# Mixture-of-experts stage: order of routing work and of the experts' first steps, and the last chunk of the combination by token tiles

## The reference, cut to what matters

```python
def _L1_ffn_ref(x, router_w, router_b, w1, b1, w2, b2, sw1, sb1, sw2, sb2):
    # N = 4096 tokens, D = 256, H = 512, E = 8 experts, S = 2 shared experts, TOP_K = 2
    xf = x.reshape(-1, D)
    sh = gelu(jnp.einsum('nd,sdh->snh', xf, sw1) + sb1[:, None, :])
    shared_out = (jnp.einsum('snh,shd->nd', sh, sw2) + sb2.sum(0)) / S
    gates = xf @ router_w + router_b
    topv, topi = jax.lax.top_k(gates, TOP_K)
    probs = jax.nn.softmax(topv, axis=-1)
    comb = jnp.einsum('nke,nk->ne', jax.nn.one_hot(topi, E, dtype=xf.dtype), probs)
    h = gelu(jnp.einsum('nd,edh->enh', xf, w1) + b1[:, None, :])
    y = jnp.einsum('enh,ehd->end', h, w2) + b2[:, None, :]
    moe_out = jnp.einsum('ne,end->nd', comb, y)
    return (shared_out + moe_out).reshape(B, L, D)
...
x = x + jnp.tanh(g_ffn[1]) * _L1_ffn_ref(_layernorm(x, axis=-1), ...)
```

## Time and profile before

| | us |
|---|---|
| median of 3 runs (1161.97 to 1167.03) | 1164.91 |
| the profiled execution, its own time | 1166.86 |
| its span in the profile | 1165.3 |
| TensorE busy in the span | 1085.4 (93%) |
| VectorE | 879.2 (75%) |
| ScalarE | 697.0 (60%) |
| GpSimd | 437.8 (38%) |

### The profile page before, as it was taken

The page is one execution under the profiler, slowest core; times in us unless marked ns, Lnnn a source line. Parts: engine busy times, 40 slices in busy tenths (PEclk is TensorE's granted clock), DMA queues, the critical chain, the costliest instruction groups (busy, mean ns, idle before and its releaser), DMA issues. The chain is left out here.

```text
span 1165.3 us, 28150 instructions
## 1 busy us (share of the span) xinstructions
PE 1085.4 (93%) x9246; PEld 932.7 (80%) x9247; DVE 879.2 (75%) x1983; ACT 697.0 (60%) x1583; POOL 437.8 (38%) x571
## 2 busy tenths in 40 slices
PE   6679998999998899999999879997999999999998
PEld 4346666989887677777776559997899999999997
DVE  8699997766676788888888538886567677666776
ACT  3478996465572566676676544465565556556553
POOL 4148884631302010111102012776523233332775
PEclk9669999999999999999999887999899999999999
DMA  9646641000005355463544015896465554455675
GB/s 323 179 156 224 224 171 56 1 0 0 0 1 115 101 126 107 90 123 79 122 93 85 3 51 214 286 329 229 151 195 174 173 173 162 170 180 168 219 235 166
DMA packets 98879, 164.81 MB, mean 141 GB/s; under 512 B 12124, under 2 KB 73404, under 8 KB 96604
## 3 DMA queue, kind: packets, MB, share of 16 engines
q1 hardware_dynamic: 89260, 137.02, 39.9%
q0 software_dynamic: 9104, 26.49, 6.8%
q10 hardware_dynamic: 416, 0.04, 0.0%
HBM read 103.76 MB, written 33.69 MB: 118 GB/s over the span
## 5 line engine op out<-in xcount | busy, mean ns | idle before, releaser
L1885 DVE TENSOR_REDUCE c_mx<-d_bank 128x2 f32<-128x512 f32 x256 | 164.4, 686 | 18.4 <-PE d_bank L2037 18.0
L1800 ACT ACTIVATE c_probs<-c_t 128x512 f32<-128x512 f32 x248 | 134.7, 598 | 27.5 <-PE c_t L2063 26.7
L2986 ACT ACTIVATE d_g_full<-d_bank,d_e_bias 128x256 f32<-128x256 f32 x156 | 77.1, 494 | 102.7 <-PE d_bank L34 102.7
L32 PE MATMUL d_bank<-de_zt_hi,d_e_hi 128*128 128x256 f32 x312 | 92.0, 295 | 2.3 <-DVE de_zt_lo L2896 2.3
L33 PE MATMUL d_bank<-de_zt_lo,d_e_hi 128*128 128x256 f32 x312 | 88.6, 284 | 0.0
L34 PE MATMUL d_bank<-d_w_hi,d_g_lo 128*128 x312 | 88.3, 283 | 0.0
L33 PE MATMUL d_bank<-d_w_lo,d_g_hi 128*128 x312 | 88.2, 283 | 0.0
L1733 POOL CAST c_ct_hi<-c_c_raw 128x512 fp32r<-128x512 f32 x15 | 9.2, 611 | 210.4 <-PE c_misc L34 210.4
L32 PE MATMUL d_bank<-d_w_hi,d_g_hi 128*128 x312 | 88.2, 283 | 0.0
L34 PE MATMUL d_bank<-de_zt_hi,d_e_lo 128*128 128x256 f32 x312 | 88.1, 282 | 0.0
L3146 POOL DMA_INDIRECT d_w_lo<-d_y_rows,d_pos x64 | 65.6, 1026 | 36.2 <-DMA d_y_rows<-de_ys 17.0
(11 more groups left out here) (428 smaller groups left out, 3786.6 us busy)
## 6 DMA issues: line engine op xcount, KB each, us to landing
d_e_raw<-in_w SPq DMA_DIRECT2D x39, 514.0 KB, 3.7
a_mb<-a_maxima SPq DMA_DIRECT2D x15, 1024.0 KB, 7.6
d_w_hi<-d_zt_kept SPq DMA_DIRECT2D x26, 512.0 KB, 4.8
d_y_rows<-de_ys SPq DMA_DIRECT2D x39, 256.0 KB, 2.1
d_z_in<-d_z_rows POOLq DMA_DIRECT2D x37, 256.0 KB, 4.2
c_kt<-c_k_hi SPq DMA_DIRECT2D x64, 128.0 KB, 3.1
c_qt<-c_q_hi SPq DMA_DIRECT2D x64, 128.0 KB, 3.7
d_zt_kept<-d_w_hi SPq DMA_DIRECT2D x20, 256.0 KB, 2.6
```

The source lines that it names most:

```text
L32: tensor.matmul(out, lhs_hi, rhs_hi, start=start, stop=False)
L1800: act.activation(probs[h % PR][:], t_bank(n, p, k), ACT.Exp).then_inc(exp_done, 1)
L1885: dve.tensor_reduce(mx[n % 2][:, :, k, p:p + 1], s_ps[h % SB], AX.X, ALU.max).then_inc(max_done, 1)
L2986: act.activation(g_full[:, m, :], hid[m][:, 0:TOK], ACT.Gelu, bias=bias[u][:, m:m + 1]).then_inc(gelu_full, 1)
```

## The change

Nothing is added to or taken from the arithmetic. What moves:

- Router products: the second one (chunk 1) is issued right behind the first, ahead of the first transposes. TensorE's ranking of group 2 comes half a chunk later.
- Ranking of group 0 on VectorE: after the low part of bank 1 of chunk 2 instead of bank 3.
- First scatters: token tile 0's two are issued ahead of the fifth reciprocal root and wait for 8 GELUs instead of 12.
- Experts' turn: on TensorE behind the output of chunk 14; on VectorE behind both splits and the output of chunk 14; on ScalarE behind both splits and the exponential.
- Bias sums: four of the eight adds of the shared bias come behind tile 2's `split_w`.
- Combination: VectorE weighs chunk 14 before the output add of chunk 13; the last chunk's output is made, added and stored by token tiles, each in a bank of its own; its last gathers wait for two GELUs fewer.

```diff
@@ moe_route, scatter() and GpSimd's order @@
-            pool.wait_ge(gelu_hi, KF * (2 * group + 3) + apart)
+            pool.wait_ge(gelu_hi, KF * (2 * group + 3) + apart if i > 0 else 2 * KF)
...
         for h in range(CHUNKS):
+            if h == 2:
+                scatter(0)
             if PT * (h + 3) < TILES:
                 rstds(h + 3)
             if h >= 2 and PT * (h - 2) < TILES:
-                for i in range(PT * (h - 2), PT * (h - 1)):
+                for i in range(max(1, PT * (h - 2)), PT * (h - 1)):
                     scatter(i)
@@ ScalarE @@
-        turn_experts(act)
         split(2)
...
         split(3)
+        turn_experts(act)
@@ VectorE @@
-                if m == 3 and h % 2 == 0 and 1 <= h // 2 <= GROUPS:
+                if m == (1 if h == 2 else 3) and h % 2 == 0 and 1 <= h // 2 <= GROUPS:
                     rank(h // 2 - 1)
...
             if h == CHUNKS - 1:
-                turn_experts(dve)
+                split(2)
+                split(3)
             if h >= 1:
                 output(h - 1)
...
-        split(2)
-        split(3)
+        turn_experts(dve)
         output(CHUNKS - 1)
@@ TensorE @@
-        gates_part(0)
+        for r in range(2):
+            gates_part(r)
...
-                if r <= CHUNKS:
+                if 2 < r <= CHUNKS:
                     gates_part(r - 1)
-                if half == 0 and h % 2 == 0 and 1 <= h // 2 <= GROUPS:
+                if half == (h + 2) // MID and h % 2 == 0 and h >= 2:
                     rank(h // 2 - 1)
...
             hidden_late(h, h % 2)
-            if h == CHUNKS - 1:
-                turn_experts(pe)
             output(h - 1, (h - 1) % 2)
+        turn_experts(pe)
         output(CHUNKS - 1, (CHUNKS - 1) % 2)
@@ moe_experts, GpSimd @@
             pool.tensor_copy(w_hi[u][:], w_raw[u][:, 0:KD * FF]).then_inc(w_hi_done, 1)
+            if isinstance(i, int) and i == AHEAD:
+                add_bias(range(E // 2, E))
...
-            for e in range(E):
+            add_bias(range(E // 2))
+
+        def add_bias(some):
+            shared = out_bias[:, E, :]
+            for e in some:
                 pool.tensor_tensor(out_bias[:, e, :], out_bias[:, e, :], shared, ALU.add).then_inc(bias_shared, 1)
@@ moe_combine @@
-                after(pool, gelu_hi, KF * n + (KF // T) * t - 1)
+                after(pool, gelu_hi, KF * n + (KF // T) * (t if n < LAST else 0) - 1)
...
+        def outputs_last(t):
+            dve.wait_ge(weighed, T * TOP * CHUNKS)
+            dve.wait_ge(last_done, t + 1)
+            xs = x_all[:, T * LAST + t, :]
+            dve.scalar_tensor_tensor(out=xs, in0=y_last[t], scalar=M.half_tanh[:, 0:1], in1=xs, op0=ALU.mult,
+                                     op1=ALU.add).then_inc(last_added, 1)
...
-        for n in range(CHUNKS + 1):
-            if n < CHUNKS:
-                hidden(n)
+        for n in range(CHUNKS):
+            hidden(n)
             if n == 0:
                 probabilities()
+            if 1 <= n < LAST:
+                weigh(n - 1)
+            if n == LAST - 1:
+                weigh(n)
             if n >= 1:
-                weigh(n - 1)
                 outputs(n - 1)
+        weigh(LAST)
+        for t in range(T):
+            outputs_last(t)
```

More of the change, by code:

```diff
@@ L3099, in moe_combine @@
     HEAD = 3
+    LAST = CHUNKS - 1
     def sem(name):
@@ L3113, in moe_combine @@
     y_done, weighed, x_added = sem("y_done"), sem("weighed"), sem("x_added")
+    last_done, last_added = sem("last_done"), sem("last_added")
+    y_last = [y[LAST % 2][:, 0, :]] + [hid[t][:, 0:D] for t in range(1, T)]
     out_tiles = out.rearrange("b (j p) d -> p (b j) d", p=P)
@@ L3125, in store, with store_last @@
             sync.dma_start(out_tiles[:, T * n:T * (n + 1), :], x_all[:, T * n:T * (n + 1), :]).then_inc(x_stored, 16)
+        def store_last(t):
+            sync.wait_ge(last_added, t + 1)
+            sync.dma_start(out_tiles[:, T * LAST + t, :], x_all[:, T * LAST + t, :]).then_inc(x_stored, 16)
         sync.wait_ge(experts.y_done, S.PAIR_TILES)
@@ L3134, in on_sync @@
                 store(n - 1)
-        store(CHUNKS - 1)
-        sync.wait_ge(x_stored, 16 * CHUNKS)
+        for t in range(T):
+            store_last(t)
+        sync.wait_ge(x_stored, 16 * (CHUNKS - 1 + T))
     def on_gpsimd(pool):
@@ L3178, in hidden, with weigh_one @@
                 dve.tensor_tensor(g_lo[n % 2][:, m, :], g_full[:, m % GR, :], g_hi[n % 2][:, m, :], ALU.subtract).then_inc(gelu_lo, 1)
+        def weigh_one(n, k, t):
+            dve.wait_ge(gathered[n % RR], 16 * T * TOP * (n // RR + 1))
+            if k > 0:
+                dve.wait_ge(weighed, T * (TOP * n + k))
+            xs = x_all[:, T * n + t, :]
+            dve.scalar_tensor_tensor(out=xs, in0=rows[n % RR][:, t * TOP + k, :], scalar=M.prob[:, T * n + t, k:k + 1], in1=xs,
+                                     op0=ALU.mult, op1=ALU.add).then_inc(weighed, 1)
         def weigh(n):
-            dve.wait_ge(gathered[n % RR], 16 * T * TOP * (n // RR + 1))
             for k in range(TOP):
-                if k > 0:
-                    dve.wait_ge(weighed, T * (TOP * n + k))
                 for t in range(T):
-                    xs = x_all[:, T * n + t, :]
-                    dve.scalar_tensor_tensor(out=xs, in0=rows[n % RR][:, t * TOP + k, :], scalar=M.prob[:, T * n + t, k:k + 1], in1=xs,
-                                             op0=ALU.mult, op1=ALU.add).then_inc(weighed, 1)
+                    weigh_one(n, k, t)
+        def outputs_last(t):
[4 more added lines that the diff above has]
+                                     op1=ALU.add).then_inc(last_added, 1)
         def outputs(n):
@@ L3221, in outputs @@
                 cols = slice(t * P, (t + 1) * P)
-                out_y = y[u][:, t, :]
+                out_y = y_last[t] if n == LAST else y[u][:, t, :]
                 for m in range(KF):
@@ L3225, in outputs @@
                                       (w2_hi[:, m, :], w2_lo[:, m, :]), m == 0, m == KF - 1)
-            mm.then_inc(y_done, 1)
+                if n == LAST:
+                    mm.then_inc(last_done, 1)
+            if n < LAST:
+                mm.then_inc(y_done, 1)
         pe.wait_ge(experts.last_lo, 1)
```

## The result

The changed kernel takes 1161.58 us in the median of 15 runs (1158.41 to 1163.94), the kernel before 1164.33 us (15 runs, 1161.4 to 1167.03): a ratio of 0.9974 with a 95% interval of 0.9965 to 0.9984, 2.75 us less. The profiled execution has a span of 1160.4 us against 1165.3.

The account below looks back on a forecast made before the run. GpSimd's scatters and its chain before expert tile 2 were taken to bound the time at which TensorE's unbroken run starts. 0.9 + 2.7 − 0.5 = 3.1 us gives 1161.8 against the median; range 1156.8 to 1165.8.

Parts of the forecast that it names:

- the scatters' term: Routing: earlier ranking and first scatters start tile 1's scatter and end the scatter chain 0.9 us earlier; bounds 0 and 1.7.
- the tail's loss: Combination's last chunk: weighing chunk 14 earlier delays the last output and final add; loss 0.5 us, within 0.2 to 1.0.
- the bias sums' 2.7: Border before tile 2: four adds behind the cast take 3.3 us off GpSimd's chain, less 0.6 for VectorE's low part.
- all later scatters ... go on back to back: GpSimd's routing scatters: later ones have several microseconds of slack to their GELU, so the 0.9 us gain carries through.
- a sign of being wrong: Routing: the prediction is wrong if the chain of scatters ends earlier by over 2 us or not at all.
- the rival with the opening's clock: Opening: the router product fills a wait, so half clock ends sooner; up to 2.6 us, time 1159.2, chance 0.10.
- my upper bound: Border: VectorE's low part of tile 2 loses at most 1.3 us, by waiting for two of GpSimd's moved adds.
- its rule of exclusion: SBUF: GpSimd and a two-SBUF-input VectorE operation exclude each other for a whole instruction; loss at most one add, 0.97 us.
- room: Border: the turn and splits bring TensorE 3.0 us earlier, worth 0 alone, only lifting the 2.30 us cap on the sums.
- The second idle time: TensorE's wait ahead of tile 2's first matmul, 2.30 us before; forecast at 2 to 3 us after the change.
- rival 1: Behind the second idle time TensorE's clock stays full, saving 1.7 us of lost work; time 1160.1, chance 0.15.
- TensorE's last output ... can start only then: Combination's tail: last output waits for chunk 14's weighing, an add and four low parts, starting at 1158.3, ending at 1161.3.

Follow-up runs that it names:

- first pair: Profiled executions of the kernel before and of the changed kernel, on a chip without TensorE's stalls; spans of 1165.3 and 1160.4 us.
- Experiment 6: Changed kernel with GpSimd waiting for VectorE's low part of tile 2's weights before its last four bias adds; 0.9969 against the kernel before.
- experiment 7: Changed kernel with the weighing of chunk 14 back in its old place, behind chunk 15's low parts; 0.9962 against the kernel before.

## Why the prediction was right, and where it was not

The time (1161.8 forecast, 1161.58 measured; gain 3.1 and 2.75) came out by errors that cancel: the scatters' term was 1.4 us too high, the border's 0.8 too low, the tail's loss 0.5 too large. That the sum is within 0.4 us is luck; of its three terms only the bias sums' 2.7, with the turn in its new place, was of the right size (the border's 3.5 less 0.8 for shorter instructions ahead of the sums, below).

**First scatters: right at the place, wrong in the sum.** Positions, first scatter and the GELU's hold went as said; tile 1's scatter came 0.7 to 1.0 us earlier, counted from the choice. The step that failed is "all later scatters ... go on back to back": they do, but each lasts as long as what stands beside it lets it, and an earlier start put the 35th just behind the start of a split (1.94 us for 1.09). The term is a loss of 0.1 to 0.9 us (0.5 in the mean of four), for a gain of 0.9; my lower bound was 0. Counted from the first choice, then, the chain of scatters ends no earlier at all, which the prediction had named as a sign of being wrong.

**Router products: 0 up to the first choice, as said**; the rival with the opening's clock fell. That the GELU which holds tile 1's scatter comes 0.65 us later with them was not seen; the scatters' 0.7 to 1.0 us has this loss in it. The ranking of group 2 gave back its 2.06 us at no effect, but a part of it stayed (0.86 at 751.52, ahead of a router product).

**Turn, splits, bias sums: sizes wrong, joined.** I priced the turn at 0 alone and the sums at 2.7. Together they are 3.5 (20.38 to 16.86). Alone, the sums are 0.94, because the low part then waits for all the adds, which is more than my upper bound (1.3 us for two adds; it is 2.6), and more than the one add, 0.97, that the prediction drew from its rule of exclusion. The turn's place was worth 2.6 to 3.0 on top (from 19.44 or 19.85 to 16.86); what it is worth without the bias split was not measured on a chip like the first pair's. The cover that I called "room" contained two things that I had not costed: VectorE's splits beside GpSimd's first two instructions (2.46 us against 1.65, the scaling 1.72 against 0.92), and whatever decides who goes first, the adds or the low part. In the changed kernel itself the low part is at 1.76, as forecast (1.8). The second idle time, 1.72, is under my 2 to 3 because GpSimd's first two instructions took 0.8 us less. From the landing to expert tile 0 it is 4.9 us, forecast at some 5.3.

**The half clock behind the second idle: open.** From tile 2 to the first gather it is 236.05, 236.11 and 236.18 us where the clock falls, 234.55 in both traces where it does not: 1.5 us, as rival 1 had it with 1.7. (Experiment 6, with a full clock too, has 235.62, with waits of its own.) The stretch right behind, first in the changed kernel, then with the weighing back:

```profile
832.00:834.00 2.00, 2.00 (x11) 2.00 (x10) 1.16 (x3) 1.44 (x3) 2.00 (x4) 0.50 0.00 0
```

```profile
832.00:834.00 2.00, 2.00 (x20) 2.00 (x19) 1.20 (x2) 1.82 (x5) 2.00 (x5) 1.00 0.00 0
```

0.50 is the lower of its two levels, 1.2 GHz, and 1.00 is 2.4 GHz. Idle times of 1.72, 2.09 and 2.30 us were followed by the lower one, others of 1.23, 1.64 and 2.09 were not. 2.09 went either way, so the length alone doesn't tell. The changed kernel's trace has the fall, so rival 1's gain is not in its 1161.97.

**Tail: the size nearly right, the path wrong.** Forecast +0.5, in the pair +0.56. But the step "TensorE's last output ... can start only then" is not on the path, as experiment 7 shows; I had read the wait of 1.44 us in the earlier trace rows and drawn nothing from it. Over all traces the new tail takes 92.20 to 93.40 us from the first gather, the old one 92.84 and 92.97, so its worth is 0 to within 0.6. Behind the last add the stores by halves do return 0.3 (3.63 to 3.32), and two adds of half a chunk cost 0.13 more than one.

With the table's means (scatters +0.5, border −3.5, tail 0) the sum is −3.0; the runs say −2.75.

**What stays open:** why the low part gets in behind the first add with the new turn and only behind the last with the old one. In both it starts 0.06 to 0.08 us after the first add. What the turn alone is worth where GpSimd is last at the border. And why two chips stall; see below.

## What to carry to other kernels

An edit that only "makes room" can be what the next one's gain hangs on: cost the pair, and run each alone and without each. Where two engines take turns at SBUF, give the later instruction's duration both ends, behind none and behind all that is queued on the other side. And when a chain is moved by a microsecond, look at which of its instructions then begin just behind a long one of a neighbour.

## What the runs showed of the hardware

On two of the three chips of the experiments the kernel before takes 34 to 35 us longer than on the third. In the eight traces taken there TensorE waits 19 to 26 us for "issue", 10 to 14 of them between 700 and 800 us and 7 to 12 from 1000 us on, when the gathers run, and under 2 elsewhere; in the first pair it is 0.9 and 1.2 us in all, none of it in these stretches. Its clock reads 0.50 for 111 to 142 us of the span there, for 90 to 108 in the six other traces. The scatters' chain grows by 12 to 15 us and the gathers' by 13 to 16. That the stalls come while GpSimd issues indirect transfers is shown; what holds TensorE is not. On such a chip the change is worth 0.9991 (0.9972 to 1.001), since the border that it mends is hidden.

An indirect scatter of GpSimd, 0.96 us alone, took 1.94 when a 128x1024 subtraction of VectorE from SBUF had just begun, and 65 of 65 scatters that began inside one with 0.17 to 1.11 us to go lost all but some 0.13 of it. The same kind of subtraction took 1.23 alone and 1.76 or 3.82 beside four adds of GpSimd, each figure always in the same kernels.
